# Neighbour sums taken one tile ahead of the search, in two PSUM banks by turns, in a two-step graph kernel

## What is computed

```python
S = S + eye(n)                       # S is adj
Rf = S / S.sum(axis=1)               # rows
Rb = S / S.sum(axis=0)[:, None]      # columns
Xf, Xb, Xa = X, X, X                 # X = relu(layernorm(x))
for s in range(2):
    A  = attention of Xa, per row cut to the logits that hold 90% of its softmax
    Xf = Rf @ Xf
    Xb = Rb @ Xb
    Xa = A @ Xa
    Z += Xf @ U1[s] + Xb @ U2[s] + Xa @ U3[s]
out = x + layernorm(X + Z) * gamma + beta
```

## Time and profile before

| | |
|---|---|
| median of 3 runs | 2169.99 us (2163.16 to 2171.1) |
| the profiled execution | 2169.9 us |
| its span, first to last instruction | 2168.2 us |
| mean granted TensorE clock | 0.956 of full speed |
| busy, share of the span | TensorE 87%, DVE 88%, ScalarE 77%, POOL 33% |
| the neighbour sums (L1519) | 2028 matmuls, 455.7 us busy, mean 380 ns |

### The profile page before, as it was taken

The page is one execution under the profiler, slowest core; times in us unless marked ns, Lnnn a source line. Parts: engine busy times, 40 slices in busy tenths (PEclk is TensorE's granted clock), DMA queues, the critical chain, the costliest instruction groups (busy, mean ns, idle before and its releaser), DMA issues. The chain is left out here.

```text
span 2168.2 us, 32420 instructions
## 1 busy us (share of the span) xinstructions
PE 1883.3 (87%) x9866; PEld 1252.5 (58%) x9866; DVE 1912.8 (88%) x6117; ACT 1678.5 (77%) x1740; POOL 711.0 (33%) x1392
## 2 busy tenths in 40 slices
PE   3999765999999999999864999989998999999992
PEld 2566433666666666666642656565655566565662
DVE  7788889988899998889748899999999999999995
ACT  5444256999999999999626899989999898989840
POOL 2000043444334444434504333333333333333324
PEclk9999987999999999999986999999999999999996
DMA  7788330111111111111125010101010010101023
GB/s 262 295 317 312 114 130 20 34 56 55 51 55 55 35 54 55 51 55 56 34 75 207 1 45 23 45 23 45 23 36 32 24 44 23 45 23 45 22 94 121
DMA packets 65725, 167.61 MB, mean 77 GB/s; under 512 B 7037, under 2 KB 45307, under 8 KB 61947
## 3 DMA queue, kind: packets, MB, share of 16 engines
q1 hardware_dynamic: 65530, 165.43, 22.0%
HBM read 117.95 MB, written 47.45 MB: 76 GB/s over the span
## 5 line engine op out<-in xcount | busy, mean ns | idle before, releaser
L1468 PE MATMUL banks<-xa,pt 128*128 128x256 f32 x2704 | 644.2, 390 | 14.5 <-ACT pt L968 13.7
L1468 PEld LDWEIGHTS banks<-xa,pt 128*128 128x128 f32 x2704 | 507.0, 194 | 158.9 <-issue 71.3
L939 ACT ACTIVATE junk_a<-pb_all,minus_t 128x3327 f16<-128x3327 f32 x150 | 461.0, 3073 | 98.9 <-POOLq L862 96.4
L944 ACT ACTIVATE junk_a<-pb_all,minus_t 128x3327 f16<-128x3327 f32 x150 | 460.6, 3071 | 4.1
L1519 PE MATMUL banks<-region,at 128*128 128x512 f16 x2028 | 455.7, 380 | 0.0
L847 POOL TENSOR_SCALAR over<-over,points 128x1 f32<-128x1 f32 x150 | 97.1, 647 | 761.0 <-ACT junk_a L944 761.0
L1519 PEld LDWEIGHTS banks<-region,at 128*128 128x128 f16 x2028 | 196.4, 98 | 217.7 <-issue 1.3
L1394 PE MATMUL banks<-keys,qs 64*128 64x512 f32 (+1 forms) x816 | 190.1, 565 | 100.7 <-DMA qs<-q_d 31.0
L1260 DVE TENSOR_SCALAR_CACHE_REDUCE pb_all<-banks 128x1024 f32<-128x1024 f32 x260 | 209.2, 848 | 31.1 <-PE banks L1394 22.6
L1122 DVE MAX8 junk_v<-below 128x8 f32<-128x208 f32 (+1 forms) x624 | 222.4, 432 | 2.2
L968 ACT ACTIVATE pt<-banks 128x896 f32<-128x896 f32 x208 | 171.1, 859 | 63.6 <-PE banks L1460 63.4
(11 more groups left out here) (221 smaller groups left out, 2738.5 us busy)
## 6 DMA issues: line engine op xcount, KB each, us to landing
at<-adjT_d SPq DMA_DIRECT2D x52, 832.0 KB, 4.9
region<-in_adj_dram SPq DMA_DIRECT2D x25, 1663.5 KB, 7.9
adjT_d<-at SPq DMA_DIRECT2D x26, 832.0 KB, 3.9
fb_d<-fb_sb SPq DMA_DIRECT2D x26, 256.0 KB, 2.0
region<-fb_d SPq DMA_DIRECT2D x2, 3328.0 KB, 17.7
y_d<-y_sb SPq DMA_DIRECT2D x50, 128.0 KB, 1.7
x_d<-pb_all SPq DMA_DIRECT2D x1, 3328.0 KB, 10.4
qs<-q_d SPq DMA_DIRECT2D x104, 32.0 KB, 4.2
```

What stands on the lines that cost most here:

```text
L939: nc.scalar.activation(junk_a[:, 0:w], pb[u][:, 0:w], ACT.Relu, scale=sign, bias=t, accum_out=over[u][:, 0:1])\
L944: nc.scalar.activation(junk_a[:, 0:w], pb[u][:, 0:w], ACT.Sign, scale=sign, bias=t, accum_out=over[u][:, 1:2])\
L1468: last = nc.tensor.matmul(bank[4][:, 0:D], pt[sl][:, t * P:(t + 1) * P], xa[:, t0 + t, :], start=(t0 + t == 0), stop=(t0 + t == T - 1))
```

## The change

The sums of tile i+1, no longer those of tile i, are made in body i, in bank 5 or 6 by the tile's slot. Their wait for `xfb` is now for the tile two before. The load of the block and the addition of the identity move forward by one body with them. In body 0 of both steps the sums (those of tile 1) come ahead of the logits of tile 2. In body 25 there are none left. The diff, cut to its core:

```diff
 SP, body(i)
-                    if j.inside(T):
-                        after(sp, "sx_psum", j + -1)
-                        sp.dma_start(at[j.slot]..., adjT_d[dyn(j)])
+                    a = i + 2
+                    if a.inside(T):
+                        after(sp, "sx_psum", a + -1)
+                        sp.dma_start(at[a.slot]..., adjT_d[dyn(a)])
 POOL, body(i), j = i + 1
-                    if i.inside(T):
-                        pool.wait_ge(S2("at_loaded")[i.slot], 16 * (i.use + 1))
-                        nc.gpsimd.tensor_tensor(at[i.slot][:, i.t, :], at[i.slot][:, i.t, :], ident16[:, :], ALU.add)\
-                            .then_inc(S2("st_ready")[i.slot], 1)
+                    if j.inside(T):
+                        pool.wait_ge(S2("at_loaded")[j.slot], 16 * (j.use + 1))
+                        nc.gpsimd.tensor_tensor(at[j.slot][:, j.t, :], at[j.slot][:, j.t, :], ident16[:, :], ALU.add)\
+                            .then_inc(S2("st_ready")[j.slot], 1)
 ACT and DVE, where the sums are read
-    bank[5]
+    bank[5 + i.slot]
 PE
+                def neighbours(i, k, j):
+
+                    if not first:
+                        pe.wait_ge(S("fb_loaded"), 32)
+                    pe.wait_ge(S2("st_ready")[j.slot], j.use + 1)
+                    pe.wait_ge(S2("xfb")[j.slot], 2 * j.use)
+                    PARTS = 1 if first else 2
+                    for n in range(PARTS):
+                        if n == 1 and k.inside(T):
+                            turn_own(k)
+                        for t in range(T):
+                            if n == 1 and t == T // 2 and i.t > 0:
+                                count_flags(i, 0)
+                            mov = parts[:, t, :] if first else parts_fb[:, t, n * 2 * D:(n + 1) * 2 * D]
+                            last = nc.tensor.matmul(bank[5 + j.slot][:, :], at[j.slot][:, t, :], mov, start=(n == 0 and t == 0),
+                                                    stop=(n == PARTS - 1 and t == T - 1))
+                    last.then_inc(S("sx_psum"), 1)
 PE, body(i), j = i + 1, k = i - 1, m = i + 2
+                    if i.t == 0:
+                        neighbours(i, k, j)
                     if m.inside(T) and (first or m.t > 0):
                         logits(m, 2 if k.inside(T) else 0, len(LCH))
...
-                        if not first and not i.inside(T):
+                        if not first and not j.inside(T):
                             turn_own(k)
-                    if i.inside(T):
...
-                        if first:
-                            count_flags(i, 0)
+                    if j.inside(T) and i.t != 0:
+                        neighbours(i, k, j)
+                    elif not first and i.t in (0, T - 1):
+                        count_flags(i, 0)
+                    if first and i.inside(T):
+                        count_flags(i, 0)
```

More of the change, by code:

```diff
@@ L1022, in body @@
                             for n, sc in enumerate((rinv, cinv)):
-                                nc.scalar.activation(t256[i.slot][:, n, :], bank[5][:, D:2 * D], ACT.Copy, scale=sc[:, i.t, :])\
+                                nc.scalar.activation(t256[i.slot][:, n, :], bank[5 + i.slot][:, D:2 * D], ACT.Copy, scale=sc[:, i.t, :])\
                                     .then_inc(S2("sx_lo")[i.slot], 1)
@@ L1026, in body @@
                             for n, (dst, sc) in enumerate(((xf_sb, rinv_s), (xb_sb, cinv_r))):
-                                nc.scalar.activation(dst[i.slot][:, :], bank[5][:, n * D:(n + 1) * D], ACT.Copy, scale=sc[:, i.t, :])\
+                                nc.scalar.activation(dst[i.slot][:, :], bank[5 + i.slot][:, n * D:(n + 1) * D], ACT.Copy, scale=sc[:, i.t, :])\
                                     .then_inc(S2("xfb")[i.slot], 1)
@@ L1230, in spread @@
                     for n, (dst, sc) in enumerate(((xf_sb, rinv), (xb_sb, cinv))):
-                        nc.vector.scalar_tensor_tensor(out=dst[i.slot][:, :], in0=bank[5][:, 0:D],
+                        nc.vector.scalar_tensor_tensor(out=dst[i.slot][:, :], in0=bank[5 + i.slot][:, 0:D],
                                                        scalar=sc[:, i.t, :], in1=t256[i.slot][:, n, :],
@@ L1438, in rest_of_z @@
                     last.then_inc(S("z_psum"), 1)
+                def neighbours(i, k, j):
[14 more added lines that the diff above has]
+                    last.then_inc(S("sx_psum"), 1)
                 def body(i):
+                    j = i + 1
                     k, m = i + -1, i + 2
```

4 lines of the change are left out of this document (2 added, 2 removed).

## The result

| | before | with the change |
|---|---|---|
| median | 2169.99 us | 2186.52 us (2178.31 to 2187.46) |
| the profiled execution's span | 2168.2 us | 2184.2 us |
| mean granted TensorE clock | 0.956 | 0.952 |
| the sums | 2028 matmuls, 455.7 us busy | 2028 matmuls, 456.4 us busy |

The ratio of the times is 1.0077 with an interval of 1.0056 to 1.0098: the change costs 16.5 us by the medians and 16.0 us by the two spans. The forecast was 2185.6 us. Both kernels give two groups of times here: the one before 2163.2 to 2164.0 us (three times) and 2170.0 to 2172.3 (four times), the changed one 2178.3 (twice) and 2185.9 to 2187.5 (five times). The medians take one value out of each mixture. By the means of the groups the change costs 14.8 us between the lower two and 15.6 us between the upper two. What parts the groups turned out to lie in the kernel itself, and is half of what follows.

A forecast was written before the change was run, and what follows sets the result against it. The prediction took a loop over DVE as the bound, through TensorE's flags and logits in step 1, with ScalarE and POOL close in step 2. Terms 11.5 + 2.5 + 1.0 + 0.7 = 15.7 on 2169.9 gave 2185.6 us, range 2177 to 2193.

The forecast's parts named there:

- Steady tiles: Middle tiles of both steps: same matmuls at the same place, so no change in time, 0 us.
- waits on the sums: ScalarE's two waits, 5.5 and 1.8 us: removing them gains 0, as ScalarE then waits for TensorE's transposes.
- work of the last tiles: Sums of tile 25 leave TensorE's last full body: gain 0, since TensorE then only waits longer for DVE.
- Start of step 2, the take: Two blocks of sums precede the logits of tile 2, so DVE takes these 14.8 us later.
- later still: Rival, chance 0.10: parts_fb or the block of tile 1 lands later at step 2's start; about 2192 us.
- Start of step 2, what comes back: In tile 1, DVE's waits of 3.77 and 2.52 us shrink: 3.3 us regained, bounds 0 and 6.3.
- Start of step 1: Without a block there TensorE idles and its clock drops, slowing transposes and products: +2.5 us, bounds 0 and 3.6.
- the two ends: Body 25 without its sums leaves TensorE gaps and slower work: +1.0 us in step 1, +0.7 in step 2.
- TensorE was not the bound: Rival, chance 0.05: TensorE's own work sets the pace, so blocks leaving the last bodies count whole; 2152.5 us.
- the second bank: Rival, chance 0.03: the waits on the sums had held the kernel up and would go; 2162.6 us.
- Caught up: Rival, chance 0.20: all 6.3 us come back in tile 1, clock holds in step 1 and ends; 2178.4 us.

The follow-up runs named there:

- guard_s2: guard_before's wait on DVE, with the sums one tile ahead in step 2 alone: 2180.14 us, 14.6 us above guard_before_2.
- guard_before_2: guard_before run again, on the same chip as guard_s1 and guard_s2: 2165.51 us.
- guard_s1: guard_before's wait on DVE, with the sums one tile ahead in step 1 alone: 2167.16 us, 1.7 us above guard_before_2.
- guard_before: Kernel before plus one wait: in step 2 from tile 1, DVE's first full-width search pass waits for POOL's second rough level of the next tile; 2165.31 us.
- guard_loads: guard_before, with step 2's load of xa issued only after parts_fb has landed and behind the queries of tile 2: 2169.58 us.

## Why the prediction was right, and where it was not

- **Steady tiles 0, waits on the sums 0, work of the last tiles 0:** right. The spacing is unchanged to 0.02 us in step 2, and the line of the sums has no waiter left.
- **Start of step 2, the take (14.8):** right in its result and its path. The addition ran at 1169.19 (forecast 1169.2), the second block from 1169.71 to 1181.1 (1169.2 to 1180.8), DVE's wait was 18.22 us (18), tile 1's search began at 1202.64 (1202). The first block began at 1155.21, not later than the 1156.8 allowed, but took 13.66 us, so that it ended at 1168.9, 0.7 us ahead of the end of the addition. One term under it was wrong without harm: I had the block of tile 1 land 2.2 us behind 1143.03. It takes 21.3 us before and 21.1 us with the change, and was there at 1167.0. Two us more, and the rival "later still" would have begun to come true.
- **Start of step 2, what comes back (3.3 of 6.3):** this step failed. I read the waits of 3.77 and 2.52 us in tile 1 as a shortage that a delay would relieve. They were the stall, an event that a delay of a few tenths of a us switches on or off and that came back one tile later in the profiled execution of the change. Without it on either side step 2 costs 14.6 us (guard_s2), and in sum nothing comes back. The traces divide most of the 14.6, counted from tile 0, whose search is 0.4 us later already. ScalarE starts the exponentials of tile 2 12.7 us later; before, it was busy until 2 us behind the take, now it waits for it. Before, then with the change:

```profile
1174.89 3.05 ACT L921 ACTIVATE pb_all<-pb_all,negmax 128x3327 f32<-128x3327 f32 x1
```
```profile
1188.03 3.07 ACT L922 ACTIVATE pb_all<-pb_all,negmax 128x3327 f32<-128x3327 f32 x1 [12.59 <-DVE negmax L1266]
```

  The guarded pair gives the same: 1188.16 in guard_s2 against 1175.41 in guard_before_2. The second part is POOL's first instruction of the last threshold of tile 1, which falls into DVE's cut now (2.15 us at 1199.96); before it took 0.27:

```profile
1186.81 0.27 POOL L847 TENSOR_SCALAR over<-over,points 128x1 f32<-128x1 f32 x1 [2.39 <-ACT junk_a L944]
```

  That would be 1.9 us, but only against this execution. In guard_before_2, which the 14.6 is counted from, the same instruction takes 1.28 us (at 1187.33), and in guard_s2 2.14: 0.9 us. Another 0.7 us is the guard itself, which holds DVE in tile 2 of guard_s2 and not of guard_before_2. The first wide pass of tile 2 is 14.6 us later there (1242.54 against 1227.97).

- **Start of step 1 (2.5) and the two ends (1.7):** mis-sized. The mechanism is there, 3.22 and 3.79 us in place of 1.72 and 3.29, but the two are worth 1.5 us at tile 2, and the ends cost nothing: the later searches there are later by what they were before. Step 1 costs 1.7 us (guard_s1), some 0.8 us of it inside the step by the traces; step 2's end costs none that the traces show.
- **The sum:** 15.7 against 16.5, and 14.2 to 15.6 where like executions are compared. That it came so near is in part luck: 3.3 us too much given back, and 4.2 us charged where about 1.7 was due at most. Against the rivals: TensorE was not the bound, the second bank paid nothing, and parts_fb was not later than taken. "Caught up" came nearest, if one looks at the two executions at 2178.3; but there the stall was missing, not the delay made good: the like executions of the kernel before are at 2163.5.
- **The chances:** by the medians the ratio is clear of half a per cent on the slower side. That the baseline had two groups 7 us apart should have widened the range: the three shown ahead of it, 2163.16 to 2171.1, held both. Its upper end was also added up wrongly: 14.8 + 3.6 and half of 3.6 and 2.2 are 21.3 us, so 2191.2, not 23 and 2193. And the middle of 0 and 6.3 is 3.15, not 3.3. Neither changes what the result says.

## What to carry to other kernels

Work that is moved ahead costs nothing only where the engine waits for nothing else: between two loads landing and the first work that a whole pipeline hangs on, 104 matmuls "in idle time" were 14.6 us, and the same block one place later cost 2.8 in both steps together. When the times of one kernel fall into two groups, profile one of each before reading any difference; here an overlap of a few tenths of a us between a short instruction and a long pass on another engine was worth 7 us, and one wait in front of the pass was a better change (guard_before, 6.0 us by the median, 0.17% by the ratio) than the one studied. Look in its trace, too, whether the wait ever waits where it is meant to. Waits in a first tile are not a reserve until one knows what makes them.

## What the runs showed of the hardware that I had not expected

- A POOL instruction of 0.3 us was held for as much of a full DVE pass as was left, 3.74 us at the longest, even when it started only 0.02 us behind the pass. What follows is larger than the hold: a tile of 43.0 to 44.6 us in place of 37.0, since the late level meets the next pass as well.
- The same TensorE work at the same place, 26 matmuls of 512 columns after the same 26.56 us of idle time, took 6.04 to 7.66 us from one execution to another, and the transposes 3 us behind it 1.72 to 3.22 us. The granted clock over 346.5 to 350.0 us was 0.81 in guard_loads (6.04 us) and 0.50 in guard_s2 (7.66 us), so it rose at different moments, and a single profile doesn't tell which of these a kernel has.
